# Sampling on 64-pixel blocks, regrouped per four image rows, with five or six candidate rows per tile

## The chip, the cores and the metric

The kernel runs on one core of a Trainium2 chip. The metric is the device time of one execution in microseconds (us); lower is better. Engines are named as in the profile: PE is TensorE's matmul, PEld its weight load, DVE is VectorE, ACT is ScalarE, POOL is GpSimd, SP issues most of the DMAs.

## What is computed

Four layers with a residual around each, on x of shape 2x192x96x96 in float32: a pair of deformable convolutions, an edge filter with a 1x1 merge, an RWKV layer and a Mamba layer. The change touches the first layer only:

```python
xr = conv1x1(gn(x), w_reduce, b_reduce)             # 192 -> 180 channels
offs = conv1x1(xr, w_offset, b_offset)              # 360: two convs, 10 groups x 9 taps x (y, x)
f_w = deform_conv2d(xr, offs[:, :180], w_dcnw, b_dcnw)
f_h = deform_conv2d(xr, offs[:, 180:], w_dcnh, b_dcnh)
# deform_conv2d: for each pixel, group and tap, sy = y + ky - 1 + dy, sx = x + kx - 1 + dx;
# val = bilinear sample of 18 channels of xr at (sy, sx), zero outside the image;
# out = einsum over taps and channels with the 3x3 weights
attn = softmax(conv1x1((f_w + f_h).mean(axis=(2, 3)), w_attn, b_attn))
x = x + conv1x1(attn[0] * f_h + attn[1] * f_w, w_expand, b_expand)
```

## The kernel before

Phases run one after the other: `first_norm_and_projections` (L153), `far_samples` (L367), `sample_and_convolve` (L652), `mix_and_expand`, and then the edge, RWKV and Mamba phases, which the change leaves alone.

**A bilinear sample as a matmul and a weighting.** A tile is 128 consecutive pixels; there are NT = 72 tiles per image and two images, 144 in all. For a tile and one of NB = 20 "samples" (two convolutions x 10 groups) each of the 9 taps needs 18 channels. The x-interpolation is a matmul: the stationary side is `HX`, for 96 image columns x 64 pixels the hat 1 - |x position - column| cut at zero; the moving side is `XW`, some image rows x 18 channels of xr over 96 columns. A tile holds pixels of two image rows, so for offsets up to 2.5 rows WIN = 6 candidate rows are taken: 6 x 18 = 108 columns. The y-interpolation is DVE's multiplication of the result by `HY`, the hats in y (`weigh`, L964 to L974). POOL adds the two halves of the six rows (`halve`, L889), DVE adds the remaining three in two steps (`quarter` L980, `sum_rows` L987). PE turns the values around (L859) and multiplies with the convolution weights (L872).

The matmul of a sample, two column halves of the array (o = 0 and 64) for the two halves of the tile:

```python
for t in range(TAPS):
    ky = t // 3
    for o in (0, 64):
        ins = e.matmul(PT[j % 2][o:o + 64, t // 3, (t % 3) * WIN * CG:(t % 3 + 1) * WIN * CG],
                       HX[:, m // 2 % RP, m % 2, t * 128 + o:t * 128 + o + 64],
                       XW[:, i, ky:ky + WIN, g * CG:(g + 1) * CG], ...)
```

**Order of the work.** Each engine has its own program, in an order written out by hand. `body` stands for four tiles (NRB = 4) and is a hardware loop of `nw` passes; nw is 1 if `far_samples` finds few enough samples with a larger offset. PE's step n (two samples a step, ten steps a tile): turn values of n; `sample(n+6)`, `sample(n+7)`; convolution matmuls of n. DVE's: `unload(n)` (copies what PE turned), a quarter of the next tile's `rows` (y distances, L934) at four of ten steps, `weigh(n+6)`, `quarter(n+4)`, `weigh(n+7)`, `sum_rows(n+4)`. PE's `sample(n+8)` waits until `weigh(n+6)` has emptied its PSUM buffer (PT has two), and the convolution matmuls wait for `unload(n)`. ACT makes the hats in x for pairs of samples, `distance` (L779) and `hats` (L784) on 96x2304 elements, seven and six pairs ahead of PE's step, and four small row-weight steps a tile (L795, L798), the first of which waits for DVE's `rows`. SP issues, for a pair, the broadcast load of the x positions into one of RP = 8 slots (`pair_load`, L743), which PE frees; before the ten pair loads of a tile stand the loads of y offsets (L724), of a distance table (L725) and of what far samples add (`CR`, L729; `KF`, L730), and among them the load of XW (L720) and the store of a finished tile (L737). POOL's `keep` (L906, L908) scales the kept sum ACC and adds CR.

**Far samples.** `far_samples` finds offsets outside the window (up to 8 candidates per partition, up to 128 in all), gathers their data with one indirect DMA per operand and adds their contribution into the `cor` array in DRAM. If there are more, nw becomes NWIN = 17 passes over all rows.

Of the kernel before, what the change touches and what calls it, by code (L numbers as in the profile page):

```python
# [18 lines left out]
NWIN = 17  # L19
# [5 lines left out]
PADT = 4  # L25
ROWS = 108
# [126 lines left out]
def first_norm_and_projections(nc, k):  # L153
# [4 lines left out]
    with Phase(nc, "in") as p:  # L158
# [34 lines left out]
        DT = p.sb([128, 3])  # L193
# [13 lines left out]
        with p.block() as blk:  # L207
            @blk.sync
            def _(e):
                for dst, src in ((WR[:, :, :], k.d["w_reduceT"].rearrange("(k p) o -> p k o", p=HC)),  # L210
                                 (WO[:, :, :, :], k.d["w_offT"].rearrange("(k p) t o -> p k t o", p=HM)),
                                 (BR[:, :], k.d["b_reduceT"]),
                                 (BO[:, :], k.d["b_offT"]), (DT[:, :], k.d["c_dlt"]), (BY[:, :], k.d["b_offy"][0:1, :].partition_broadcast(128)), (KX[:, :], k.d["c_kx"]), (PXR[:, :], k.d["c_pxr"])):
# [5 lines left out]
                for b in range(B):  # L219
                    for r0 in (0, PADT + H, PADT + H + 4):  # L220
                        e.dma_start(k.xr_v[b][r0:r0 + 4].rearrange("r p c -> p r c"), Z[:, :, :]).then_inc(s_zs, 16)
                for c, (b, r) in enumerate(chunks):
# [13 lines left out]
                e.wait_ge(s_zs, 16 * (6 + 2 * N)).then_inc(s_zs, -16 * (6 + 2 * N))  # L236

            @blk.scalar
            def _(e):
# [7 lines left out]
                def size(c):  # L247
# [3 lines left out]
                    for u in range(3):  # L251
                        ins = e.activation(AB[:, c % 3, u * CM:(u + 1) * CM], OY[:, c % 2, u, :], ACT.Abs,
                                           bias=DT[:, u:u + 1])
# [61 lines left out]
            def _(e):  # L315
                e.memset(Z[:, :, :], 0.0).then_inc(s_z, 1)
                for q in range(2):
                    e.sem_inc(s_st1[q], 16)
                    e.sem_inc(s_sx[q], 32)
# [13 lines left out]
                for c in range(N):  # L333
# [10 lines left out]
                    e.wait_ge(s_sx[q], 32).then_inc(s_sx[q], -32)  # L344
# [10 lines left out]
                for q in range(2):  # L355
                    e.wait_ge(s_st1[q], 16).then_inc(s_st1[q], -16)
                    e.wait_ge(s_sx[q], 32).then_inc(s_sx[q], -32)
# [9 lines left out]
def far_samples(nc, k):  # L367

    BIG = 1000.0
    SPARE = float(B * HW * 2)  # L370
    with Phase(nc, "far") as p:
        IOTA = p.sb([128, 8 * NCH0])
        PART = p.sb([128, 1])
        TRI = p.sb([128, 2, 128])
# [4 lines left out]
        CIF = p.sb([128, 8 * NCH0])  # L379
        EQ = p.sb([128, NCAND, 8 * NCH0])  # L380
# [4 lines left out]
        OH = p.sb([128, NCAND, 128])  # L385
        FL = p.sb([1, 4])
        Q = p.sb([128, 48])
        IN = p.sb([128, 1], I32)
        AD = p.sb([128, 8], I32)
        YX = p.sb([128, 2])  # L390
        XV = p.sb([128, 4, CG])
        WG = p.sb([128, CG * CM])
        WP = p.sb([128, CG * CM])
        VL = p.sb([128, CG])
        OUT = p.sb([128, CM])
        SUMS = p.sb([128, CM])
        RD = p.sb([128, 128])
        EM = p.sb([128, 128])
        EL = p.sb([128, 128])
# [3 lines left out]
        (s_w, s_v, s_cn, s_tot, s_oh, s_pay, s_ad, s_ix, s_rd, s_r, s_em, s_o, s_go) = p.sems(13)  # L403
# [2235 lines left out]
```

## Time and profile before

| what | us |
|---|---|
| median of 3 runs | 12407.22 (12399.02 to 12415.76) |
| profiled execution, its own time | 12423.67 |
| its span | 12421.6 |
| projections, about 86 to 455 | 369 |
| far samples and start of sampling, 455 to 548 | 93 |
| sampling, 548 to 7575 | 7027 |
| mix and expand, 7575 to 7837 | 262 |
| the other three layers, 7837 to the end | 4584 |

Busy over the span: PE 11555.8 us (93%), weight loads 8928.9 (72%), DVE 10330.4 (83%), ACT 10361.2 (83%), POOL 5958.3 (48%). How to read the rows: an instruction in float32 is issued as two on PE, so the 51,948 matmuls of L831 are 103,896 rows. The duration of one matmul is a latency that overlaps the next; what a stream costs is the distance of the starts. The rows on which the prediction rests stand further down.

### The profile page before, as it was taken

Reading aid. Unit: us, or ns where it says so; the run is one execution under the profiler, and the core shown is the slowest. Engines: PE = TensorE matmul, PEld = TensorE weight load, DVE = VectorE, ACT = ScalarE, POOL = GpSimd, SP = SyncE. Lnnn points to the kernel's source line nnn. Section 1 sums busy time; section 2 is a strip of 40 time slices with the busy share of each in tenths; the row PEclk is TensorE's granted clock in tenths of the full one; section 3 lists DMA queues with packets and bytes.
Section 4 is the critical chain, followed back from the end, with each engine's and each line's share of the span. In section 5 each row is a group of like instructions: output and inputs, shape, how many; then the busy total and the mean of one; then the engine's idle time right before and its main releaser. Section 6 shows DMA issues by size and latency. Waiting matters only on the chain. (4 is left out here: it accounts for less than half of the span.)

```text
span 12421.6 us, 338253 instructions
## 1 busy us (share of the span) xinstructions
PE 11555.8 (93%) x133056; PEld 8928.9 (72%) x133056; DVE 10330.4 (83%) x13907; ACT 10361.2 (83%) x10330; POOL 5958.3 (48%) x3910
## 2 busy tenths in 40 slices
PE   7699999999999999999999999880699899999999
PEld 4599999999999999999999996430533355555555
DVE  5588888888888888888888886799878788888888
ACT  3499899899998998989989885397768899899988
POOL 0155554455444545445454451033300388888887
PEclk9899999999999999999999997895899899999999
DMA  6688888888888888888888888444644333333332
GB/s 181 164 209 206 208 205 203 204 206 208 204 204 201 208 206 207 206 200 208 206 207 205 202 206 210 140 155 139 178 130 159 127 99 108 102 100 107 99 103 85
DMA packets 850969, 2144.79 MB, mean 173 GB/s; under 512 B 108322, under 2 KB 447184, under 8 KB 707168
## 3 DMA queue, kind: packets, MB, share of 16 engines
q1 hardware_dynamic: 833904, 2090.65, 63.7%
q10 hardware_dynamic: 15120, 30.71, 0.7%
q8 instruction: 1080, 17.69, 0.6%
q14 instruction: 481, 3.94, 0.1%
q0 software_dynamic: 384, 1.79, 0.0%
HBM read 1827.33 MB, written 295.56 MB: 171 GB/s over the span
## 5 line engine op out<-in xcount | busy, mean ns | idle before, releaser
L831 PE MATMUL dc_p<-dc_t 96*64 96x108 f32 x103896 | 5162.5, 257 | 85.9 <-issue 44.9
L831 PEld LDWEIGHTS dc_p<-dc_t 96*64 96x64 f32 x103896 | 4847.6, 136 | 353.6 <-issue 351.7
L900 POOL TENSOR_TENSOR dc_t<-dc_t 128x486 f32<-128x486 f32 x2885 | 3169.6, 1099 | 3525.6 <-DVEq L990 2344.8
L972 DVE TENSOR_TENSOR dc_t<-dc_p,dc_t 128x972 f32<-128x972 f32 x2886 | 3367.5, 1167 | 976.0 <-DVEq L970 880.4
L779 ACT ACTIVATE dc_t<-dc_t 96x2304 f32<-96x2304 f32 x1447 | 3191.8, 2206 | 222.3 <-ACTq L778 219.0
L784 ACT ACTIVATE dc_t<-dc_t 96x2304 f32<-96x2304 f32 x1446 | 3049.7, 2109 | 0.0
L2481 DVE TENSOR_TENSOR_SCAN ms_t<-ms_t,ms_p 128x512 f32<-128x512 f32 x1728 | 2128.5, 1271 | 282.9 <-PE ms_p L2423 203.5
L2397 POOL TENSOR_TENSOR ms_t<-ms_t 128x1536 f32<-128x1536 f32 x576 | 1987.9, 3457 | 503.5 <-DVE ms_t L2481 499.7
L2433 PE MATMUL ms_p<-ms_t,top_t 128*128 128x512 f32 x3456 | 1774.7, 596 | 0.0
L2423 PEld LDWEIGHTS ms_p<-top_t,ms_t 128*128 128x128 f32 x6912 | 849.7, 141 | 967.6 <-issue 693.1
L872 PE MATMUL dc_p<-dc_t 128*128 128x180 f32 (+1 forms) x7488 | 1537.0, 337 | 0.6 <-PEq L867 0.3
L872 PEld LDWEIGHTS dc_p<-dc_t 128*128 128x128 f32 (+1 forms) x7488 | 1139.2, 190 | 201.4 <-issue 4.0
L2369 ACT ACTIVATE ms_t<-ms_t 128x384 f32<-128x384 f32 x2304 | 1222.5, 603 | 24.2 <-PE ms_p L2423 24.2
L2376 ACT ACTIVATE ms_t<-ms_t 128x512 f32<-128x512 f32 x1728 | 1114.3, 709 | 0.0
L2423 PE MATMUL ms_p<-top_t,ms_t 128*128 128x128 f32 x6912 | 1048.3, 274 | 57.5 <-DVE ms_t L2481 51.1
L992 DVE TENSOR_TENSOR dc_t<-dc_t 128x324 f32<-128x324 f32 x1442 | 823.1, 571 | 0.0
L984 DVE TENSOR_TENSOR dc_t<-dc_t 128x324 f32<-128x324 f32 x1442 | 702.0, 487 | 0.2 <-DVEq L982 0.2
L959 DVE COPY dc_t<-dc_p 128x256 f32<-128x256 f32 (+1 forms) x1440 | 673.4, 468 | 9.1 <-DVEq L954 8.7
L859 PE MATMUL dc_p<-top_t,dc_t 128*128 128x128 f32 (+1 forms) x3744 | 646.3, 273 | 0.2 <-PEq L856 0.2
L795 ACT ACTIVATE dc_t<-dc_t 128x540 f32<-128x540 f32 x290 | 187.4, 646 | 535.3 <-ACTq L793 513.0
L934 DVE TENSOR_TENSOR dc_t<-dc_t 128x270 f32<-128x270 f32 x580 | 557.8, 962 | 71.6 <-DVEq L932 69.7
L2433 PEld LDWEIGHTS ms_p<-ms_t,top_t 128*128 128x128 f32 x3456 | 522.2, 191 | 15.8 <-DVE ms_t L2491 11.5
(256 smaller groups left out, 9864.2 us busy)
## 6 DMA issues: line engine op xcount, KB each, us to landing
dc_t<-sxd SPq DMA_DIRECT2D x1447, 864.0 KB, 5.9
ms_t<-bcd SPq DMA_DIRECT2D x576, 256.0 KB, 3.3
dc_t<-xrT SPq DMA_DIRECT2D x145, 540.0 KB, 9.0
kvd<-wk_t SPq DMA_DIRECT2D x18, 1536.0 KB, 5.1
szd<-mi_t SPq DMA_DIRECT2D x36, 768.0 KB, 4.4
xvd<-mi_t SPq DMA_DIRECT2D x36, 768.0 KB, 4.8
dld<-mi_t SPq DMA_DIRECT2D x36, 768.0 KB, 3.4
ms_t<-dld SPq DMA_DIRECT2D x36, 768.0 KB, 6.7
```

Source lines behind the costliest of these rows:

```text
L779: e.activation(HX[:, q % RP, :, :], HX[:, q % RP, :, :], ACT.Abs, bias=QX[:, 0:1]).then_inc(s_ab, 1)
L784: e.activation(HX[:, q % RP, :, :], HX[:, q % RP, :, :], ACT.Relu, bias=1.0, scale=-1.0)\
L831: ins = e.matmul(PT[j % 2][o:o + 64, t // 3, (t % 3) * WIN * CG:(t % 3 + 1) * WIN * CG], HX[:, m // 2 % RP, m % 2, t * 128 + o:t * 128 + o ...
L872: ins = e.matmul(PF[:, conv * CM:(conv + 1) * CM], VT[0:o, n // 2 % 2, u, :], WD[0:o, c, conv, :], start=(c == 0), stop=(c == NCK - 1), sk ...
L900: e.tensor_tensor(ZH[:, n % 4, :, :], z[:, :, 0:HALF], z[:, :, HALF:2 * HALF], ALU.add)\
L972: e.tensor_tensor(Zt[:, n % 4, :].rearrange("p (b m i) -> p b m i", b=3, i=CG), PT[n % 2][:, :, 0:3 * WIN * CG].rearrange("p b (m i) -> p ...
L2369: ins = e.activation(BU[:, i % RT, tb, :], UT[:, c % 2, tb, 0:DI], ACT.Copy, scale=UT[:, c % 2, tb, DI + n:DI + n + 1])
L2376: ins = e.activation(DA[:, i % RA, d, :], DL[:, c % 2, d, :], ACT.Exp, scale=AL[:, d, n:n + 1])
L2397: e.tensor_tensor(G[:, i % RG, :, :], HH[:, i % RH, :, :], CB[:, i % RB, :].unsqueeze(1).to_broadcast([128, ND, T]), ALU.mult).then_inc(s_ ...
L2423: ins = e.transpose(PB[:, d, tb * 128:(tb + 1) * 128], BU[:, i % RT, tb, d * 128:(d + 1) * 128], k.ident[:, :])
L2433: e.matmul(PY[:, d, :], k.ident[:, :], G[:, i % RG, d, :], start=(n == 0), stop=(n == NS - 1))\
L2481: e.tensor_tensor_scan(HH[:, i % RH, d, :], DA[:, i % RA, d, :], PB[:, d, :], CAR[:, n, d:d + 1], ALU.mult, ALU.add).then_inc(s_scan, 1)
```

## The change

**Tiles.** The 384 pixels of four image rows are six blocks of 64. Before, a tile is two neighbouring blocks: every tile touches two image rows. Now TILES pairs blocks (0, 2), (3, 5) and (1, 4). Blocks 0, 2, 3 and 5 each lie in a single image row; blocks 1 and 4 cross one. The first two tiles of three take five candidate rows (90 columns in place of 108), the third six. The two halves of a tile now read different rows of XW (BASES). XW holds ten rows for three tiles and is loaded once per three, in place of eight rows for each.

**Loop body.** NRB goes from 4 to 12 tiles, so the loops are 12 in place of 36.

**Sums.** `CR`, `KF` and POOL's `keep` go. `sum_load` loads ACC itself from `cor` and `sum_store` writes it back, one store of 180 KB per tile more; the load stands where CR's load stood. y offsets come in two DMAs of 64 partitions.

**Reach.** For single-row blocks the window covers offsets up to 2.0 either way (the test scales |dy| by 1.25), for the others as before. `far_samples` takes up to 256 in place of 128: most steps are made for two columns, gathers are doubled, there is one more gather (`c_spot`, where a pixel stands in its tile) that DVE waits for, one of the two big products goes to POOL, and both big sums stay on DVE. NWIN becomes 21.

**Around it.** The x positions are stored in six DMAs of 256-byte runs per chunk in place of two of 512-byte runs; four more stores of zero rows. `mix_and_expand` puts pixels back in order: four ACT instructions in place of two per chunk, six DVE instructions in place of two, over the same elements.

The core of the diff:

```diff
+TILES = ((0, 2), (3, 5), (1, 4))
+BASES = ((0, 1), (2, 3), (0, 2))
+ROWSOF = (5, 5, 6)
...
-                    for conv in range(2):
-                        e.dma_start(k.d["sxd"][b, 3 * r:3 * r + 3, conv].rearrange("i k x -> k i x"),
-                                    SX[:, q, conv, :].rearrange("k (i x) -> k i x", i=3)).then_inc(s_sx[q], 16)
+                        for i, (one, two) in enumerate(TILES):
+                            e.dma_start(k.d["sxd"][b, 3 * r + i, conv].rearrange("k (a x) -> k a x", a=2),
+                                        SX[:, q, conv, :].rearrange("k (n x) -> k n x", x=64)[:, one:two + 1:two - one, :])\
+                                .then_inc(s_sx[q], 16)
...
-    NRB = 4
+    NRB = 12
...
-                def kept_loads(i, b, ti, y):
-                    e.dma_start(CR[:, i, :], k.cor_v[DS(b * NT + y, 1)].rearrange("a p c -> (a p) c")).then_inc(s_cr[i % 2], 16)
-                    e.dma_start(KF[:, i:i + 1],
-                                k.d["c_keep"][DS(ti, 1)].rearrange("a p c -> (a p) c")).then_inc(s_cr[i % 2], 16)
+                def sum_load(i, at):
+                    e.wait_ge(s_sb, 16).then_inc(s_sb, -16)
+                    e.dma_start(ACC[:, i % 3, :, :].rearrange("p v c -> p (v c)"), k.cor_v[at]).then_inc(s_cr[i % 3], 16)
...
-                            if q == 0:
-                                tile_load(i, b, first)
+                            if q == 0 and i % 3 == 0:
+                                chunk_load(i, b, e.snap(near * (4 * (y // 3) + PADT - 6) + w * STEP + 3))
                             if q == 3:
...
                                 store_tile(i, done, s_st[i % 2])
+                                sum_store((i - 2) % 3, done)
...
-                        ky = t // 3
-                        for o in (0, 64):
-                            ins = e.matmul(PT[j % 2][o:o + 64, t // 3, (t % 3) * WIN * CG:(t % 3 + 1) * WIN * CG],
+                        for h in range(2):
+                            o, first = 64 * h, BASES[i % 3][h] + t // 3
+                            ins = e.matmul(PT[j % 2][o:o + 64, t // 3, t % 3 * nr * CG:(t % 3 + 1) * nr * CG],
                                            HX[:, m // 2 % RP, m % 2, t * 128 + o:t * 128 + o + 64],
-                                           XW[:, i, ky:ky + WIN, g * CG:(g + 1) * CG],
+                                           XW[:, i // 3 % 2, first:first + nr, g * CG:(g + 1) * CG],
...
-                    e.tensor_tensor(ZH[:, n % 4, :, :], z[:, :, 0:HALF], z[:, :, HALF:2 * HALF], ALU.add)\
+                    e.tensor_tensor(ZH[:, n % 4, :, 0:m], z[:, :, 0:m], z[:, :, nr * CG - m:nr * CG], ALU.add)\
                         .then_inc(s_half, 1)
-
-                def keep(i):
...
+                for h in range(2):
+                    gather(SPOT[:, h, :], k.d["c_spot"], 0, h, s_sp)
...
                 e.wait_ge(s_ix, 1)
-                for n in range(4):
-                    gather(XV[:, n, :], k.d["xrT"][0:B * ROWS].rearrange("r x (g i) -> (r x g) i", i=CG), 4 + n, s_xv)
+                for h in range(2):
+                    for n in range(4):
+                        gather(XV[:, h, n, :], k.d["xrT"][0:B * ROWS].rearrange("r x (g i) -> (r x g) i", i=CG), 4 + n, h, s_xv)
+                e.wait_ge(s_vl, 1)
+                e.wait_ge(s_wg, 32)
+                e.tensor_tensor(WP[:, 1, :].rearrange("p (i o) -> p i o", i=CG), WG[:, 1, :].rearrange("p (i o) -> p i o", i=CG),
+                                VL[:, 1, :].unsqueeze(2).to_broadcast([128, CG, CM]), ALU.mult).then_inc(s_wp, 1)
...
+                chained(e.tensor_reduce(OUT[:, 0, :], WP[:, 0, :].rearrange("p (i o) -> p o i", i=CG), AX.X, ALU.add))
+                e.wait_ge(s_wp, 1)
+                e.tensor_reduce(OUT[:, 1, :], WP[:, 1, :].rearrange("p (i o) -> p o i", i=CG), AX.X, ALU.add)\
+                    .then_inc(s_em, 1)
```

On PE, in the middle of the sampling loop, the order is the same and the width of L831's matmuls differs. `64x108` is 64 pixels by 6 x 18 columns. Before:

```order
L831 MATMUL dc_p<-dc_t 64x108 x36
L872 MATMUL dc_p<-dc_t 128x180 x3
L859 MATMUL dc_p<-top_t,dc_t 128x128 x2
L859 MATMUL dc_p<-top_t,dc_t 84x128
L831 MATMUL dc_p<-dc_t 64x108 x36
```

After, in a five-row tile:

```order
L884 MATMUL dc_p<-dc_t 64x90 x36
L925 MATMUL dc_p<-dc_t 128x180 x3
L912 MATMUL dc_p<-top_t,dc_t 128x128 x2
L893 MATMUL dc_p<-top_t,dc_t 90x128 x2
L884 MATMUL dc_p<-dc_t 64x90 x36
```

Nothing moved in it; 90 columns stand in place of 108. On SP, the DMAs of one tile in the loop, before (`sxd` are the pair loads, `xrT` is XW, `fd` the finished tile):

```order
L724 DMA dc_t<-oyd 128x180
L725 ISA
L725 DMA dc_t<-c_tab 128x6
L729 DMA dc_t<-cor 128x360
L730 ISA
L730 DMA dc_t<-c_keep 128x1
L743 DMA dc_t<-sxd 96x2304
L720 ISA
L720 DMA dc_t<-xrT 96x8x180
L743 DMA dc_t<-sxd 96x2304 x3
L737 DMA fd<-dc_t 90x4x128
L743 DMA dc_t<-sxd 96x2304 x6
```

After, a tile with the load of XW, the first of three:

```order
L772 DMA dc_t<-oyd 64x180 x2
L773 ISA
L773 DMA dc_t<-c_tab 128x6
L778 DMA dc_t<-cor 128x360
L794 DMA dc_t<-sxd 96x2304
L766 ISA
L766 DMA dc_t<-xrT 96x10x180
L794 DMA dc_t<-sxd 96x2304 x3
L784 DMA fd<-dc_t 90x4x128
L788 DMA cor<-dc_t 128x360
L794 DMA dc_t<-sxd 96x2304 x6
```

The table's load (`c_tab`) now stands behind two loads of y offsets, `c_keep` is gone, and the store into `cor` stands behind that of `fd`.

## Rows read from the trace of the kernel before

**Rows 1.** Stages: us, engines' busy us (PE, PEld, DVE, ACT, POOL), clock, DMA share, GB/s.
```profile
86.00:455.00 369.00, 360.85 (x1632) 233.04 (x1632) 188.24 (x386) 155.98 (x336) 0.00 (x0) 1.00 0.64 185
455.00:548.00 93.00, 6.35 (x24) 5.42 (x24) 49.97 (x154) 8.68 (x7) 7.84 (x8) 0.50 0.36 97
548.00:7575.00 7027.00, 6973.47 (x115704) 6487.65 (x115704) 5983.18 (x9079) 6337.75 (x3467) 3505.31 (x3173) 1.00 0.82 205
7575.00:7837.00 262.00, 249.88 (x412) 111.78 (x412) 152.97 (x306) 64.09 (x98) 0.09 (x1) 0.50 0.87 211
```

**Rows 2.** Groups by form, 548 to 7575 us: busy us, mean ns, idle before.
```profile
L831 PE MATMUL dc_p<-dc_t 96*64 96x108 f32 x103896 | 5162.5, 257 | 85.9 <-issue 44.9 <-PEq L827 39.6
L831 PEld LDWEIGHTS dc_p<-dc_t 96*64 96x64 f32 x103896 | 4847.6, 136 | 353.6 <-issue 351.7
L972 DVE TENSOR_TENSOR dc_t<-dc_p,dc_t 128x972 f32<-128x972 f32 x2886 | 3367.5, 1167 | 976.0 <-DVEq L970 880.4
L779 ACT ACTIVATE dc_t<-dc_t 96x2304 f32<-96x2304 f32 x1445 | 3187.4, 2206 | 217.2 <-ACTq L778 213.9 <-issue 0.3
L900 POOL TENSOR_TENSOR dc_t<-dc_t 128x486 f32<-128x486 f32 x2885 | 3169.6, 1099 | 3525.6 <-DVEq L990 2344.8 <-POOLq L896 891.2 <-POOLq L899 153.1
L784 ACT ACTIVATE dc_t<-dc_t 96x2304 f32<-96x2304 f32 x1446 | 3049.7, 2109 | 0.0
...
L795 ACT ACTIVATE dc_t<-dc_t 128x540 f32<-128x540 f32 x288 | 186.1, 646 | 450.8 <-ACTq L793 428.6 <-ACTq L791 22.3
```

**Rows 3.** Timeline of PE, one step of sampling: start us, us from first to end.
```profile
5015.25 3.55 PE L831 MATMUL dc_p<-dc_t 96*64 96x108 f32 x72
5018.73 1.18 PE L872 MATMUL dc_p<-dc_t 128*128 128x180 f32 x6
...
5020.06 3.55 PE L831 MATMUL dc_p<-dc_t 96*64 96x108 f32 x72
```

**Rows 4.** Timeline of PE in the projections, matmuls of other widths.
```profile
299.91 0.63 PE L300 MATMUL in_p<-top_t,in_t 90*128 90x90 f32 x6
300.38 2.75 PE L282 MATMUL in_p<-in_t 90*90 90x384 f32 x8
302.96 1.99 PE L291 MATMUL in_p<-in_t 90*128 90x180 f32 x12
304.79 2.75 PE L274 MATMUL in_p<-in_t 96*90 96x384 f32 x8
```

**Rows 5.** Timeline of weight loads: the first four of a run of samples.
```profile
3001.41 0.20 PEld L831 LDWEIGHTS dc_p<-dc_t 96*64 96x64 f32 x4 [0.17 <-issue]
```

**Rows 6.** Waits of PE, DVE and ACT, 560 to 7570 us: total us, times, longest.
```profile
PE dc_p L831 <- issue: 44.2, 45, 2.6
...
DVE dc_t L934 <- DVEq L932: 60.5, 81, 2.1
...
ACT dc_t L795 <- ACTq L793: 428.6, 144, 3.8
```

**Rows 7.** DMA issues, 1000 to 7000 us: count, KB each, median us to landing.
```profile
dc_t<-sxd SPq DMA_DIRECT2D x1233, 864.0 KB, 5.9
...
dc_t<-c_tab SPq DMA_DIRECT2D x124, 3.0 KB, 5.3
```

**Rows 8.** Timeline of SP: one load of y offsets is issued.
```profile
523.98 0.33 SPq L724 DMA_DIRECT2D dc_t<-oyd  x1
```

**Rows 9.** Groups in the far phase, 455 to 548 us.
```profile
L432 POOL DMA_INDIRECT far_t<-xrT,far_t x4 | 3.8, 944 | 11.9 <-DVE far_t L611 11.0 <-issue 0.9
L422 PE MATMUL far_p<-far_t 128*128 128x4 f32 x16 | 3.6, 355 | 11.5 <-DVE far_t L502 11.5
```

**Rows 10.** Timeline of DVE in the far phase, the end of its chain.
```profile
502.32 0.24 DVE L457 TENSOR_SCALAR far_t<-far_t 128x18 f32<-128x18 f32 x1 [4.44 <-DMA far_t<-xrT,far_t]
...
503.41 3.53 DVE L463 TENSOR_TENSOR far_t<-far_t 128x3240 f32<-128x3240 f32 x1
506.98 6.77 DVE L633 TENSOR_REDUCE far_t<-far_t 128x180 f32<-128x3240 f32 x1
```

More of the change, by code:

```diff
@@ L419, in _ @@
                 e.matmul(PA[:, 2:4], ONES[:, :], CN[:, :], start=True, stop=True).then_inc(s_tot, 1)
                 e.wait_ge(s_oh, 1)
-                for n in range(NCAND):
-                    ins = e.matmul(PB[:, 0:4], OH[:, n, :], PAY[:, n, :], start=(n == 0), stop=(n == NCAND - 1))
+                for h in range(2):
+                    for n in range(NCAND):
+                        ins = e.matmul(PB[:, 4 * h:4 * h + 4], OH[:, n, h * 128:(h + 1) * 128], PAY[:, n, :],
+                                       start=(n == 0), stop=(n == NCAND - 1))
@@ L445, in _ @@
[L445 removed]
+                for h in range(2):
+                    e.indirect_dma_start(k.d["cor"], bass.IndirectOffsetOnAxis(ap=AD[:, 8, h:h + 1], axis=0), SUMS[:, h, :],
+                                         None).then_inc(s_cor, 16)
+                e.wait_ge(s_cor, 32)
             @blk.vector
@@ L550, in _ @@
-                floor(delta, t0, t1)
-                pairs(delta, delta, u, ALU.subtract)
-                scale(spare, PART[:, :], 1.0, SPARE)
-                combine(row, px, 2.0, conv)
+                scale(spare, PART[:, :], 1.0, SPARE)
+                tile, place, base, delta, centre, reach = (SPOT[:, :, n] for n in range(6))
+                e.wait_ge(s_sp, 32)
+                combine(row, c, 3.0, tile)
+                combine(t1, row, 2.0, conv)
+                combine(t1, t1, float(HM), gt)
@@ L635, in _ @@
                 scale(t1, b, -1.0, 1.0)
+                pairs(ey, t1, t0, ALU.mult)
+                pairs(sx, t1, conv, ALU.mult)
+                pairs(dy, b, t0, ALU.mult)
+                pairs(dx, b, conv, ALU.mult)
+                e.wait_ge(s_xv, 128)
+                for h in (1, 0):
+                    scale(VL[:, h, :], XV[:, h, 0, :], ra[:, h:h + 1], None, ALU.mult, ALU.bypass)
+                    combine(VL[:, h, :], XV[:, h, 1, :], rb[:, h:h + 1], VL[:, h, :])
+                    combine(VL[:, h, :], XV[:, h, 2, :], xa[:, h:h + 1], VL[:, h, :])
+                    ins = e.scalar_tensor_tensor(out=VL[:, h, :], in0=XV[:, h, 3, :], scalar=xb[:, h:h + 1],
+                                                 in1=VL[:, h, :], op0=ALU.mult, op1=ALU.add)
+                    if h == 1:
+                        ins.then_inc(s_vl, 1)
+                    else:
+                        chained(ins)
@@ L2620, in layout @@
-    d["c_dlt"] = (pu // W - np.arange(3) - REACH + 2).astype(f)
+    block, base, single = (np.zeros((3, 2, 64), np.int64) for _ in range(3))
+    for i in range(3):
+        for h in range(2):
+            block[i, h], base[i, h], single[i, h] = TILES[i][h], BASES[i][h], ROWSOF[i] == 5
+    at = (64 * block + np.arange(64)).reshape(3, 128)
+    base, single = base.reshape(3, 128), single.reshape(3, 128)
+    row = at // W
+    r = np.arange(WIN)
+    tab = np.zeros((2, H // 4, 3, NWIN, 128, WIN), f)
```

402 lines of the change are left out of this document (216 added, 186 removed).

## Prediction, made before the changed kernel was run

> **What bounds the kernel now.** I read the stages first [rows 1]. Sampling takes 7027 us of 12421.6, and in it PE is busy 6973 us, ACT 6338, DVE 5983, POOL 3505, with the DMA engines at 0.82. So per tile (7027 / 144 = 48.8 us) PE has almost no air; ACT fills 6338 / 144 = 44.0 us, DVE 41.5. The groups by form [rows 2] say what PE does there: the 103,896 issued matmuls of L831, 36 per sample. The waits confirm the bound from the other side: DVE and ACT wait for their turn [rows 2, 6], while PE's L831 has 85.9 us of idle time in the stage, 44.2 of them put down to "issue" in 45 gaps.
>
> A busy PE need not be a PE that is bound by columns, so I read distances of starts. One step, two samples, is 72 instructions in 3.55 us [rows 3]. Without the last one's latency (257 ns, rows 2) that is 3.29 / 71 = 46.4 ns each, 92.8 ns per pair, a pair being the instruction of the left half and that of the right. In the projections, where a matmul uses the whole array width, the starts give 0.47 / 6 = 78 ns for 90 columns, 1.83 / 12 = 152.5 for 180 and 2.58 / 8 = 322.5 for 384 [rows 4]: 2.5 ns + 0.833 ns per column. For 108 columns that line gives 92.5 ns. So two halves together cost what one costs alone, the weights are loaded under the stream, and the columns set the pace. The clock is at its upper level, 2.4 GHz, in this stage (1.00 in rows 1). A whole step lasts 4.81 us [rows 3], ten make 48.1 us a tile; the last 0.7 us of the 48.8 are the start and scattered stalls.
>
> **Sampling matmuls.** Width 108 becomes 90 in two tiles of three, 96 tiles. By the line a pair goes from 92.5 to 77.5 ns; the 78 ns for exactly 90 columns [rows 4] stands for it too. 15 ns x 18 pairs = 0.27 us per sample, x 20 = 5.4 us per tile, x 96 = **518 us** off PE's path. A five-row tile then takes 42.7 us on PE, a six-row tile 48.1, the mean is 44.5.
>
> Could the weight loads hold the pace? In the trace four loads, 136 ns each [rows 2], fit into 0.20 us [rows 5], so two pairs start within 64 ns: a pair of loads can follow every 55 to 64 ns, under 77.5. I take the columns. The Trainium skill (TensorE: Matmul & The Clock Gate, section "LDWEIGHTS (loading the stationary operand)") gives a load about its columns / 1.2 in ns, 53 for 64 columns. Two of them in turn would be 107 ns per pair, and the narrower matmul would save nothing (the second rival's 12,435 us); the trace, at 92.8 per pair, disagrees with loads in turn and agrees with loads of both halves side by side.
>
> **What is late next.** ACT: 44.0 us per tile; its small steps shrink from 540 to 450 elements, by the slope between 2304 and 540 elements (2109 and 646 ns, rows 2) 75 ns each, 0.3 us a tile. So it needs 43.7 in a five-row tile against PE's 42.7, 44.0 in a six-row one against 48.1. In three tiles it needs 131.4 us, PE 133.5. Its 428.6 us of waiting at L795 [rows 6], 3 us a tile, are where it stands ahead of DVE's `rows`; it is three pairs, about 12.8 us, ahead of PE there and loses 2 us of that in two tiles. So it hides, narrowly: 0.7 us a tile. DVE: 41.5 us less 20 products shortened by 162 elements, at (3.53 - 1.167) / (3240 - 972) = 1.04 us per thousand elements [rows 2, 10] 0.17 each, gives 38.1 of 42.7. POOL halves 324 for 486 elements and loses `keep`; it had air. DMA: 10.0 MB a tile by rows 1 (205 GB/s x 48.8 us). XW falls from 540 to 675 / 3 = 225 KB, the store of ACC adds 180, its load replaces CR's: 9.87 MB in 44.5 us, a share of 0.82 x 0.987 x 48.8 / 44.5 = 0.89. A pair load lands in 5.9 us [rows 7] and has about six steps of 4.3 us, less some 8 us for ACT and its order; hidden.
>
> **The wait that grows.** DVE's first `rows` of a tile waits for the table, which lands 5.3 us after its issue [rows 7]: 60.5 us in 81 tiles [rows 6], 0.4 us a tile. One more issue of 0.33 us [rows 8] stands ahead of it now, and PE's step is 0.54 us shorter, so it is late by up to 1.3 us. Behind it on DVE stands `weigh(n+6)`, for which PE's sample two steps on waits. DVE's idle time shrinks from 976 / 1440 = 0.68 us a step [rows 2] to 4.6 / 10 = 0.46. One step can't absorb 1.3 us, but PE needs the result only a step later. Bounds: 0, and 0.9 us per five-row tile (all but one step's air), 86 us. With the "issue" gaps (44 us now, with more DMA load perhaps twice) I take 40 us in all, nearer to 0 since the order gives DVE a step of lead, and 0 to 130 for the range.
>
> **Sums and loop.** `sum_load` waits for the store of the tile before, issued seven pair loads (30 us) earlier: no wait. Behind it on SP stand pair loads with the air above. POOL's `keep` was hidden. 24 loop ends fewer: nothing in the trace shows that one costs PE, 0, at best a part of the 44 us.
>
> **Far samples**, an exposed chain while PE is idle (6.35 of 93 us busy, rows 1). Doubling adds: four more gathers before the wait of 4.44 us, 0.94 and 0.3 of issue each [rows 9, 10], 5.0 us; 16 more candidate matmuls, 3.6 [rows 9]; a second reduction on DVE, 6.8 [rows 10]; four small products, 1.0, four more sums of 180 elements at 0.34, 1.4, the wider one-hot, 1.1 (at 1.04 per thousand); one more scatter, 1.25; one more constant, about 1; DVE's new waits for `c_spot` and for the second address, between 0 and 4.4 each, 3.4 together. The second product, on POOL, 3240 x 1.099 / 486 = 7.3 us, is under DVE's own 3.5 + 6.8. Sum 24.6, **25 us**, range 15 to 40. The samples are a matter of data: worked out from the inputs, 119 lie outside the new windows (67 the old ones), at most 6 in one partition; 256 and 8 are allowed. It stays one pass.
>
> **Projections.** PE is busy 361 of 369 us [rows 1]. SP issues four more stores per 7.5 us chunk, at 0.33 to 0.85 us: room. DMA: x positions are 270 of 1390 KB per chunk; even if their share tripled, 0.64 would become 0.88. Hidden, but at the end some 2 us. The Trainium skill (DMA: Bandwidth & Descriptors, section "Specifications") wants 512 bytes and more per transfer and has smaller ones do a read-modify-write, which speaks against runs of 256; no row here shows such a store, and by the bound above it would stay hidden. **Mixing**: PE is busy 250 of 262 us at clock 0.50, DVE 153, ACT 64 [rows 1]. Four more DVE instructions per chunk at a fixed 0.16 us (the line above at 0 elements) are 0.6 of 2.3 us of idle time: 0. Start of sampling: 1 us.
>
> **Sum.** -518 + 40 + 25 + 2 + 1 = -450 us. On the profiled execution, 12423.7, that is 11974; it stands 16.5 us above the median of the runs, so **11957 us**, 3.6% faster.
>
> **Rivals.**
> - *The wait that grows and ACT, uncovered.* ACT's lead or DVE's step doesn't hold: each lost 0.3 to 0.9 us per tile, together 43 to 130 more than I took: 12,000 to 12,090. For it: 0.7 us of air on ACT, 0.46 on DVE. Against it: the leads. 21%.
> - *Something else than columns sets the pair.* Then only the added work is left: 12407 + 28 = 12,435, slower. It decides from a pair of 91.7 ns on, where 34,560 pairs save less than 28 us. Against it: the straight line through 78, 152.5 and 322.5, and 92.8 on it. 5%.
> - *The halves no longer run side by side*, since they read different rows of XW where they read the same. Pairs of 155 and 185 ns: 22.5 and 33.3 us more per tile, mean 26.1, 16,200 us. The starts in rows 3 are of the same rows, so no row excludes it. 2%.
> - *Too many far samples*: 21 passes. The count excludes it; with all else 1%.
> - *More than the columns.* The start and the stalls shrink, or mixing runs at the upper clock, where DVE would bound it at 0.16 us x 192 + 153 = 184 us: 11,840 to 11,905. 9%.
>
> **How the numbers follow.** My forecast with its neighbourhood, 11,905 to 12,000: 62%. Range: 11,885 to 12,055, which leaves out the slower ones and the edges of the two near ones. 0.2% is 25 us, about what a measurement of this kernel can tell from no change. Faster by more: 62 + 21 + 9 = 92%; within: 2% (part of the second rival); slower: 6%.
>
> **What would show it.** Right: L884's 72 instructions of a five-row step in about 3.0 us (71 x 38.8 + 0.25); sampling near 6550 us, five-row tiles 43, six-row 48; ACT's wait at its first row weight nearly gone; the far stage near 118 us. Wrong: the run of 72 at 3.5; PE waiting for the x hats or for `weigh`'s buffer; gaps put down to "issue" well above 80 us.

## The result, and the profile after

| | before | after |
|---|---|---|
| median of the runs, us | 12410.11 (12399.02 to 12415.76) | 12071.65 (12053.83 to 12096.23) |
| profiled execution, us | 12423.67 | 12053.83 |
| its span, us | 12421.6 | 12051.9 |

The change makes the kernel 2.7% faster: the ratio is 0.973, with a 95% interval from 0.971 to 0.9749. The direction was forecast, the size was not. 12071.65 us lies 115 us above the predicted 11957 and 17 us beyond the end of the range.

The stages of the kernel after, in the form of [rows 1] (us, busy us of PE, PEld, DVE, ACT and POOL, granted clock, DMA share, GB/s):

```profile
88.00:505.00 417.00, 381.71 (x1632) 238.00 (x1632) 190.88 (x386) 172.69 (x336) 0.00 (x0) 0.97 0.61 167
505.00:631.00 126.00, 11.99 (x46) 10.63 (x46) 67.44 (x166) 7.84 (x7) 22.94 (x19) 0.50 0.31 86
631.00:7219.00 6588.00, 6474.64 (x115704) 6009.03 (x115704) 5426.72 (x9080) 6287.46 (x3467) 2591.75 (x2885) 0.99 0.84 216
7219.00:7482.00 263.00, 249.88 (x412) 111.83 (x412) 177.58 (x497) 90.75 (x194) 0.00 (x0) 0.51 0.88 210
```

Sampling is 439 us shorter, mixing is what it was, and the two stages ahead of sampling are longer than in [rows 1]: the projections by 48 us, the far samples by 33. So the sum of the prediction can be laid beside the two profiled executions, stage by stage:

| stage | predicted, us | measured, us |
|---|---|---|
| load of x and statistics | 0 | +1.6 |
| projections | +2 | +47.4 |
| far samples | +25 | +33.5 |
| start of sampling | +1 | +0.5 |
| sampling, first to last product on DVE | -518 + 40 | -439.2 (7023.0 to 6583.8) |
| mixing | 0 | +1 |
| code that the change doesn't touch | 0 | -14 |
| sum | -450 | -370 |

The remaining 34 us of the miss of 115 have nothing to do with a mechanism. The prediction took the profiled execution as 16.5 us above the median of its runs; that of after stands 18 below its own. The row of untouched code is scatter between executions: over the changed kernels' profiles it lies between -3 and -18 us.

**The columns.** PE's groups in sampling, and one five-row step of its timeline (start us, us from first to end):

```profile
L884 PE MATMUL dc_p<-dc_t 96*64 96x90 f32 x69152 | 2935.2, 242 | 90.0 <-issue 54.3 <-PEq L879 34.1
L884 PE MATMUL dc_p<-dc_t 96*64 96x108 f32 x34560 | 1713.7, 257 | 18.0 <-issue 17.4 <-PEq L879 0.3
```

```profile
3007.04 3.01 PE L884 MATMUL dc_p<-dc_t 96*64 96x90 f32 x72
```

The 72 instructions take 3.01 us where [rows 3] has 3.55. (3.01 - 0.24) / 71 is 39.0 ns each, 78 per pair, as the line through [rows 4] said. The halves still run side by side though they now read different rows of XW. The best tiles last 42.6 and 42.9 us with five rows, 47.7 with six, and 48.0 before.

**What stands around them.** The waits in sampling, 640 to 7215 us, in the form of [rows 6]:

```profile
DVE dc_t L979 <- DVEq L977: 240.9, 143, 8.7
```

```profile
ACT dc_t L847 <- ACTq L845: 177.2, 126, 3.3
ACT dc_t L831 <- ACTq L830: 98.1, 124, 3.9
```

L979 is `rows`, DVE's y distances, and L977 its wait for the y offsets and the table; L847 is the first of ACT's row weights, which waits for `rows`, and L831 ACT's `distance`, which waits for a pair load. `rows` waited 60.5 us in 81 tiles [rows 6]; it now waits 240.9 in 143 of 144. The idle time of PE's two groups above is 108 us, from 85.9 [rows 2]; these are only the gaps that the profile sees. ACT is busy for 6287 of the stage's 6588 us, so at this point it could as well be ACT that holds the pace. That is what the second group of experiments separates.

**The projections.** SP's queue in one chunk of 384 pixels, first of before, then of after:

```profile
304.50 0.40 SPq L231 DMA_DIRECT2D xrT<-in_t  x1
304.94 1.02 SPq L234 DMA_DIRECT2D sxd<-in_t  x2
306.00 0.93 SPq L226 DMA_DIRECT2D cor<-in_t  x2
306.97 0.70 SPq L228 DMA_DIRECT2D oyd<-in_t  x1
```

```profile
301.38 0.98 SPq L235 DMA_DIRECT2D xrT<-in_t  x1
302.41 5.34 SPq L239 DMA_DIRECT2D sxd<-in_t  x6
307.79 1.03 SPq L230 DMA_DIRECT2D cor<-in_t  x2
308.87 0.44 SPq L232 DMA_DIRECT2D oyd<-in_t  x1
```

Before, SP issues for 3.2 us and then waits for the next chunk. After, it issues back to back: from xrT at 301.38 to the next xrT at 309.43 are 8.05 us, while PE needs 7.46 for a chunk. DVE's operation L353, which makes the x positions, waits for the chunk's buffer, filled two chunks earlier and not yet stored. Its waits, 110 to 480 us:

```profile
DVE in_t L353 <- DVEq L351: 109.1, 46, 4.4
```

L351, named here, is the wait for PE's result; it stands just behind L350, the wait for the buffer. From the fifteenth chunk on L351 passes 0.11 us after L350 (309.21 and 309.10 us in the chunk above), so there it is the buffer that ends last.

The stage's extra 47 us come apart by the starts of DVE's copy L349 (L343 before), 48 of each. The first comes 5 us later than the 1.6 of the load explain, and the second another 6.4 later; in this stretch PE's matmuls run at half their pace (last section). Over the following chunks the distance is 7.46 us for thirteen chunks and 8.16 on average for the 33 from then on, some 25 us more than before in all. At the end, 20 us in place of 9 lie between the last copy and the far stage, since SP is behind.

### The profile page after: what moved, and what is told of

It is laid out like the page before. It is cut to its first block and busy times, and to the rows that moved or that the text cites. A ratio compares the mean times of both kernels' runs of the same rounds, so it can differ in the third digit from the quotient of the medians.

```text
span 12051.9 us, 337397 instructions
## 1 busy us (share of the span) xinstructions
PE 11074.3 (92%) x133078; PEld 8457.9 (70%) x133078; DVE 9815.6 (81%) x14111; ACT 10353.3 (86%) x10426; POOL 5059.6 (42%) x3633
## 5 line engine op out<-in xcount | busy, mean ns | idle before, releaser
L884 PE MATMUL dc_p<-dc_t 96*64 96x90 f32 (+1 forms) x103896 | 4658.9, 247 | 144.9 <-issue 71.7
L884 PEld LDWEIGHTS dc_p<-dc_t 96*64 96x64 f32 x103896 | 4370.8, 136 | 418.1 <-issue 416.4
L955 POOL TENSOR_TENSOR dc_t<-dc_t 128x324 f32<-128x324 f32 (+1 forms) x2885 | 2591.8, 898 | 4028.3 <-DVEq L1043 2738.2
L1019 DVE TENSOR_TENSOR dc_t<-dc_p,dc_t 128x810 f32<-128x810 f32 (+1 forms) x2886 | 3043.5, 1055 | 896.4 <-DVEq L1016 861.1
L831 ACT ACTIVATE dc_t<-dc_t 96x2304 f32<-96x2304 f32 x1447 | 3189.0, 2204 | 105.6 <-ACTq L830 104.5
L1045 DVE TENSOR_TENSOR dc_t<-dc_t 128x324 f32<-128x324 f32 x1442 | 730.8, 507 | 0.0
L979 DVE TENSOR_TENSOR dc_t<-dc_t 128x225 f32<-128x225 f32 (+1 forms) x580 | 410.2, 708 | 250.6 <-DVEq L977 250.4
L912 PEld LDWEIGHTS dc_p<-top_t,dc_t 128*128 128x128 f32 (+1 forms) x3744 | 496.2, 140 | 18.9 <-issue 1.4
L1034 DVE TENSOR_TENSOR dc_t<-dc_t 128x324 f32<-128x324 f32 x962 | 465.2, 484 | 0.4 <-issue 0.2
```

What stands on the lines that cost most here:

```text
L831: e.activation(HX[:, q % RP, :, :], HX[:, q % RP, :, :], ACT.Abs, bias=QX[:, 0:1]).then_inc(s_ab, 1)
L884: ins = e.matmul(PT[j % 2][o:o + 64, t // 3, t % 3 * nr * CG:(t % 3 + 1) * nr * CG], HX[:, m // 2 % RP, m % 2, t * 128 + o:t * 128 + o + 6 ...
L912: ins = e.transpose(PR[0:o, u * 128:(u + 1) * 128], VA[:, n // NG % 2, 128 * c:128 * c + o], k.ident[:, :])
L955: e.tensor_tensor(ZH[:, n % 4, :, 0:m], z[:, :, 0:m], z[:, :, nr * CG - m:nr * CG], ALU.add)\
L1019: e.tensor_tensor(Zt[:, n % 4, 0:nr * LEN].rearrange("p (b m i) -> p b m i", b=3, i=CG), PT[n % 2][:, :, 0:3 * nr * CG].rearrange("p b (m ...
```

## Experiments

Two theories stood at each of two places. All kernels are the changed one with one edit, unless told otherwise. Medians are compared with 12071.65 us for the changed kernel; ratios are to the kernel before, on the same chip.

### What sets a chunk of the projections

**p_zeros_act.** The same stores, but two of a chunk's ten are issued by ACT:

```diff
 SyncE:   for c, (b, r) in enumerate(chunks):
 ...
-             for i in (2 * c, 2 * c + 1):
-                 e.dma_start(k.cor_z[i], Z...).then_inc(s_zs, 16)
 ScalarE:
+         e.wait_ge(s_z, 1)...
          for c in range(N):
+             for i in (2 * c, 2 * c + 1):
+                 e.dma_start(k.cor_z[i], Z...).then_inc(s_zs, 16)
```

> The changed kernel, with the two zero stores of the sums of every chunk (96 in all) issued by ScalarE in place of SyncE; the same packets go the same way at about the same time. Theory A (SyncE's time for issuing its DMAs sets the chunk in the projections: 0.97 + 6 x 0.87 + 0.57 + 0.42 + 0.44 us and gaps, 8.03 in all, against 7.46 that TensorE needs): the sum falls to about 7.0, the period of a chunk returns to 7.46, and the projections end some 25 to 30 us sooner, near 477 in place of 505.6; the time falls by as much, to about 12045. Theory B (the DMA engines set it, with twice as many descriptors of 256 bytes in place of 512): the period stays at 8.0 to 8.1 and the time at 12070.

Measured: 12039.45 us (12032.78 to 12056.33), ratio 0.9704 (0.9683 to 0.9725). The distance of the chunks is 7.46 us from the first to the last. The projections end at 461.3 us in place of 506.2, 45 us sooner; 12 of them are the slow start, which this execution didn't have. Against the kernel before, the stage is 4 us longer.

```profile
88.00:450.00 362.00, 360.60 (x1632) 232.84 (x1632) 183.93 (x375) 167.90 (x334) 0.00 (x0) 1.00 0.67 189
```

PE is busy 360.6 of 362 us again, and the DMA engines move 189 GB/s in place of 167. The same packets, issued from two queues, go through faster. Each of the six stores still holds SP for 0.87 us, though SP now pauses in every chunk, so that figure isn't one of a crowded queue. So it was SP's issue time, theory A, and not the DMA engines.

**p_two_stores.** DVE writes the x positions in the order of the tiles, and two stores take the place of six:

```diff
-    for i, (one, two) in enumerate(TILES):
-        e.dma_start(sxd[b, 3 * r + i, conv] (k, a, x), SX[:, q, conv] blocks one and two)
+    e.dma_start(sxd[b, 3 * r:3 * r + 3, conv] (k, i, x), SX[:, q, conv] (k, i, x))
```

> The changed kernel, with the x offsets of a chunk laid in the order of the tiles by VectorE (6 operations of 128 columns in place of 2 of 384), so that two stores with runs of 512 bytes take the place of six with runs of 256. Theory A: SyncE's issues come to about 3.5 us a chunk, the period returns to 7.46, the projections end near 462 to 470 (the four added stores of zero rows stay), and the time falls by 36 to 44 us, to about 12030. Theory B gives the same here, since the descriptors are halved as well; a period above 7.46 would mean that neither holds and that the larger VectorE work or something else sets it. Far samples and sampling are unchanged by either.

Measured: 12039.68 us (12029.21 to 12050.96), ratio 0.9704 (0.9684 to 0.9724). The distance is 7.46, and the projections end at 455.7 us. DVE's 25 us of extra work in the stage (209.0 of 362 us busy) cost nothing. This edit alone would not have told the theories apart. It shows that SP's 36 us can be had back; that the other 11 are missing here too is chance, since best_a has the same stores and the slow start, and its stage is 12 us longer than before.

The two traces have sampling stages of 6605 and 6599 us, 21 and 15 longer than the profiled execution of after, and the medians fell by 32 where the stage gave 45 and 50. What lengthened sampling there was not tried; with the loads early as well, in best_a, it takes 6462 us, so the two stores don't do it by themselves.

### What sets the five-row tiles

**s_early_rows.** The loads for `rows` of tile i + 1 stand behind the fifth pair load of tile i in place of behind its tenth:

```diff
-    row_loads(i, b, ti, y)
+    if i == 0:
+        row_loads(i, b, ti, y)
     sum_load(i, 2 + b * NT + y)
     for q in range(10):
         pair_load((10 * i + q) % RP, b, y, q)
+        if q == 4 and i + 1 < NRB:
+            row_loads(i + 1, b, e.snap(t0 + w + (y + 1) * NWIN), y + 1)
```

> The changed kernel, with the y offsets and the row table of a tile (three DMAs) issued five pairs earlier, in 132 of 144 tiles. Theory C (in sampling these loads land too late for VectorE's row sums, which hold up VectorE and through it ScalarE's row weights and TensorE): VectorE's wait at the row sums falls from 241 us to under 40, ScalarE's wait for them from 177 to under 60, sampling from 6584 us to about 6450 (144 tiles at the best seen, 42.6 and 47.7, are 6379), and the time by 100 to 150. Theory D (ScalarE's own work, 43.7 us a tile on average against TensorE's 44.3, sets it; its waits are those of an engine that could not have gone ahead): the waits move elsewhere and the time falls by less than 30.

Measured: 11944.97 us (11942.5 to 11957.15), ratio 0.9628 (0.9609 to 0.9648), 127 us less. Sampling takes 6467 us. The same waits, now over 700 to 6900 us (in that window the changed kernel has 221.8 at `rows` and 169.6 at ACT's row weights):

```profile
ACT dc_t L834 <- ACTq L833: 85.6, 102, 2.9
ACT dc_t L850 <- ACTq L848: 78.7, 58, 3.0
PE dc_p L887 <- issue: 30.5, 45, 1.7
...
DVE dc_t L982 <- DVEq L980: 11.1, 11, 1.8
```

The wait at `rows` is left in 11 tiles, those at the head of the loop whose loads the edit doesn't move. PE's gaps, and ACT's wait for the row sums, went with it. That is theory C; 117 of the 127 us are in sampling.

**s_less_act.** ACT's second pass works on half of the elements (every second sample's column weights are left out):

```diff
-    e.activation(HX[:, q % RP, :, :], HX[:, q % RP, :, :], ACT.Relu, bias=1.0, scale=-1.0)
+    e.activation(HX[:, q % RP, 0, :], HX[:, q % RP, 0, :], ACT.Relu, bias=1.0, scale=-1.0)
```

> The changed kernel with the second of ScalarE's two passes over a pair's columns made on half of them; the column weights of every second sample are left out by that. ScalarE has some 10 us less work in a tile. Theory D (ScalarE's work): tiles of five rows come to the best seen, 42.6 us, and sampling to about 6400, 150 to 190 us less. Theory C (late loads alone): VectorE's wait at the row sums stays near 240 us and sampling falls by less than 60. If both have a part, between the two.

Measured: 12072.49 us (12046.73 to 12094.0), ratio 0.9733 (0.9712 to 0.9755); sampling 6583.9 us against 6583.8.

```profile
ACT dc_t L831 <- ACTq L830: 1072.4, 790, 4.7
...
ACT dc_t L847 <- ACTq L845: 373.9, 136, 4.3
DVE dc_t L979 <- DVEq L977: 228.2, 134, 4.3
```

ACT now stands still for nearly a quarter of that window, and not a microsecond comes of it. Its full timetable was no bound: it was busy because it was ahead. Theory D falls.

**s_early_less_act**, both edits, asks the same of what the early loads left over.

> The changed kernel with the early loads and with ScalarE's second pass on half the columns (the column weights of every second sample are left out). What the early loads left above the floor is 6467 - 6379 = 88 us. Theory D2 (with the loads in time, ScalarE, which stands still for only 168 of 6467 us, is what is left): sampling falls by 50 to 90 more, to about 6400, and the time to 11870. Theory E (the rest is TensorE's own gaps and VectorE's order): sampling stays at 6455 to 6470 and the time at 11945.

Measured: 11949.06 us (11932.83 to 11963.21), ratio 0.9625 (0.961 to 0.964); sampling 6467.8 us. ACT is not the rest either. The five- and six-row tiles at their best, 44.4 us on average, would make 6405 us (144.25 tiles from first to last product, an estimate from the trace); some 62 us stay above that. By position in the loop they are spread over all tiles, 0.1 to 0.8 us each. What makes them was not found.

**s_six_rows.** All tiles with six rows, the regrouping kept:

```diff
     def depth(n):
-        return ROWSOF[n // NB % 3]
+        return WIN
```

and the same in `row_weights` and `rows`, with one row more in XW.

> The changed kernel with six rows on all three tiles (the weights of the sixth row are zero where the change leaves it out): the regrouping, its stores, loads, sums in memory and far samples stay, the 15% fewer columns go. If the gain of sampling is that of the columns alone and the regrouping is free, sampling takes what it took before, 7023 us, within 30, at 48.0 a tile at best, and the time is 12071 + 439 = 12510, slower than before by 0.8%. If the new loads cost something of their own besides, sampling takes 7060 to 7130. Theory C says that the wait at the row sums is much smaller here than 241 us, 60 to 120, since a pair takes 0.5 us longer and the loads have more time.

Measured: 12468.54 us (12460.76 to 12471.47), ratio 1.0039 (1.0024 to 1.0055). Sampling takes 6986 us, 37 less than before, with best tiles of 48.0. Of the 42 us by which my figure was too high 37 are these; the rest is not accounted for.

```profile
DVE dc_t L979 <- DVEq L977: 104.7, 116, 2.5
```

This run takes the sampling term apart. Against a floor of 144.25 tiles of 48.0 us, 6924, the kernel before had 99 us of stalls and this one 62: regrouping is no cost but a small gain. Six rows to five lowers the floor by 519 us, to 6405, and raises the stalls from 62 to 179. The early loads take them back to 62. So the lateness of these loads cost 117 us. By this account nearly all of it appeared only with the shorter step, though the third DMA was there with six rows too, and with it 104.7 us of wait at `rows` (49.2 in the kernel before, same window). Six rows with the loads early, which would have shown this directly, was not run.

**before_early** puts the loads five pairs earlier in the kernel before, in three of four tiles.

> The kernel before, with the y offsets and the table loaded five pairs earlier in three of four tiles. Theory C, that the load's lateness was there before and the shorter tile uncovered it: the wait at the row sums (60.5 us) nearly goes, and sampling falls by no more than those 60, likely 20 to 50, to about 6985; the time to about 12375. If the lateness came only with the change (a third DMA in a row's loads), nothing moves: 12410.

Measured: 12383.39 us (12369.2 to 12402.43), ratio 0.9972 (0.9959 to 0.9985); sampling 6986 us, 37 less.

```profile
DVE dc_t L937 <- DVEq L935: 15.1, 22, 1.9
```

The lateness was there before the change. Over 560 to 7570 us the wait falls from 60.5 [rows 6] to 16.4, and sampling gets 37 us shorter for these 44.

**s_one_pair** moves the loads by one pair only (`q == 8` in place of `q == 4`).

> The changed kernel with the loads of y offsets and table only one pair earlier (ahead of the last pair's load of the tile before) in place of five. If lateness is all there is to it, a step of 4.3 us covers most of a wait that is 1.7 us a tile on average and 8.7 at worst: the wait at the row sums falls from 236 us to 20 to 60, sampling from 6584 to 6470 to 6510, and the time to about 11965 to 11990. If the five pairs did something else besides (spread the loads away from the chunk's load and the stores, which stand at fixed places of the tile), one pair gives less than half of the 127 us.

Measured: 11947.99 us (11942.65 to 11962.35), ratio 0.9624 (0.9607 to 0.9642); sampling 6462.6 us.

```profile
DVE dc_t L982 <- DVEq L980: 9.0, 12, 1.4
```

One step of 4.3 us gives everything that five give (124 us and 127, with overlapping intervals). I had taken the wait as the lateness in every tile, with 8.7 us at worst, and so expected a rest of 20 to 60 us; but the 8.7 us is one tile at the start of the stage, and elsewhere the longest is 4.6.

**s_one_load.** The two DMAs of y offsets become one over both blocks:

```diff
-    for h in range(2):
-        at = 384 * (y // 3) + 64 * TILES[y % 3][h]
-        e.dma_start(OYT[64 * h:64 * h + 64, i % 2, :], k.oyd_v[b][at:at + 64])
+    src = k.oyd_v[b][384 * (y // 3):384 * (y // 3) + 384].rearrange("(n x) c -> n x c", x=64)
+    e.dma_start(OYT[:, i % 2, :], src[one:two + 1:two - one])
```

> The changed kernel with the y offsets of a tile loaded by one DMA over both halves in place of two, at their old place. With six rows the new loads waited 105 us where the kernel before waited 60.5, so the third DMA is put at some 45 us of wait: if it is its issue (0.55 us) and landing in a row that counts, the wait at the row sums falls from 236 to 150 to 200 us, sampling by 30 to 70 us and the time to about 12020. If the same bytes land as late through one DMA, nothing moves: wait 220 to 250, 12070.

Measured: 12386.8 us (12348.44 to 12399.3), ratio 0.9971 (0.9961 to 0.9982). This is 315 us slower than the changed kernel, and both of my expectations were wrong. Sampling takes 6880 us, and even the best five-row tile lasts 44.2.

```profile
DVE dc_t L979 <- DVEq L977: 471.1, 131, 5.0
ACT dc_t L847 <- ACTq L845: 439.4, 130, 5.7
PE dc_p L884 <- PEq L879: 221.7, 167, 3.2
```

The packets of 720 bytes say why. In one tile of the changed kernel the two DMAs' 128 packets start within 1.05 us (3034.25 to 3035.3), with 7 under way at a time. In this kernel the 128 packets of the tile at 3037 us take from 3041.3 to some 3044, with 2.2 under way at a time on average. The Trainium skill (DMA: Bandwidth & Descriptors, section "Why a DMA increments its semaphore by 16 and not by 1") has the rule: the number of engines is the largest up to 16 that divides the slowest dimension of both sides. The slowest dimension of this DMA's source is 2, so it would use two of the 16 DMA engines; with two DMAs it is 64, which 16 divides. The trace agrees, with 2.2 packets under way against 7. (It doesn't say on which engine a packet ran.)

**s_one_load_early** asks whether the two crowded engines do harm beyond the late data.

> The changed kernel with the y offsets of a tile in one DMA and, with the table, five pairs earlier. The one DMA at the old place cost 315 us. Theory F (its data only land later, since its 128 packets go two at a time and take 2.7 us in place of 1.05, and the row sums wait for them): issued five pairs earlier, the lateness is gone, the wait at the row sums is under 20 us, sampling 6465 us and the time 11945, as with two DMAs. Theory G (the packets crowded on few DMA engines hold up the pair loads behind them): the wait at the row sums goes, but the pair loads stay late, the best tile stays above 43.5 us and the time is 12050 to 12250.

Measured: 11945.67 us (11932.52 to 11956.86), ratio 0.961 (0.9592 to 0.9627); sampling 6470 us, best tiles of 42.6 again. Theory F holds: all 315 us were the wait at `rows`. In the one at the old place that wait is 3.6 us a tile (471.1 over the 130 tiles of the window) where the changed kernel has 1.6 (221.8 over 136), and the 2.0 us of difference are the 2.1 by which a tile is longer there. A DMA whose data are not awaited may be as clumsy as this one for nothing.

### All together

**best_a**: early loads, two stores, and the far samples' second product on DVE.

```diff
 GpSimd:
-    e.wait_ge(s_vl, 1)
-    e.tensor_tensor(WP[:, 1], WG[:, 1], VL[:, 1] broadcast, ALU.mult).then_inc(s_wp, 1)
 VectorE, ahead of the second reduction:
-    e.wait_ge(s_wp, 1)
+    pairs(WP[:, 1], WG[:, 1], VL[:, 1] broadcast, ALU.mult)
```

> The changed kernel with three edits together: the y offsets and the table of a tile five pairs earlier, the x offsets stored with two DMAs a chunk in the order of the tiles, and the second product of the far samples on VectorE in place of GpSimd. If the gains add: 127 us of the early loads, some 44 of the stores (projections end 50 us sooner in that trace), and 2 of the product (3.5 us on VectorE in place of the 5.5 us for which its 0.24 us operation stood still beside GpSimd's product), so 11945 - 44 - 2 = about 11900. If ScalarE or the queue takes part of one of them back, 11915 to 11945. In the far stage itself: if VectorE stands still because of GpSimd's operation, the step from the loaded values to the last sum falls from 24.5 us by about 2; if the 5.5 us were a wait for something else, it rises by 3.5.

Measured: 11902.9 us (11896.65 to 11904.68), ratio 0.9586 (0.9573 to 0.9599). It beats both kernels, by 507 and 169 us (517 against the kernel before on its own chip). The gains add up. In its far stage, from the loaded values to the last reduction:

```profile
531.23 0.24 DVE L482 TENSOR_SCALAR far_t<-far_t 128x18 f32<-128x18 f32 x1 [7.26 <-DMA far_t<-xrT,far_t]
...
533.41 3.53 DVE L488 TENSOR_TENSOR far_t<-far_t 128x3240 f32<-128x3240 f32 x1
536.97 6.77 DVE L673 TENSOR_REDUCE far_t<-far_t 128x180 f32<-128x3240 f32 x1
543.78 3.53 DVE L488 TENSOR_TENSOR far_t<-far_t 128x3240 f32<-128x3240 f32 x1
547.34 6.77 DVE L676 TENSOR_REDUCE far_t<-far_t 128x180 f32<-128x3240 f32 x1
```

From 531.23 to the end of the last reduction the step takes 22.9 us where it took 24.5: DVE does 3.5 us more work and is done 1.6 us sooner.

## Why the prediction was wrong

The miss is 115 us. The projections make 45 of them, the stalls of sampling 39, the far samples 8.5, the level of the medians 34; the small terms and the untouched layers take 12 back.

**The bound and the columns: right.** PE and its columns set sampling. The term was 518 us; the best tiles of six-row and five-row kernels are 519 apart over the stage. A pair of 77.5 ns was forecast, 78 found; the rivals of another bound and of halves in turn are excluded.

**The projections: the step that failed.** "SP issues four more stores per 7.5 us chunk, at 0.33 to 0.85 us: room." The room was never added up. With SP's own issues before (0.40 + 1.02 + 0.93 + 0.70, some 3.2 us with its gaps) four more at 0.85 would have made 6.6 of 7.46, so even the sum would have said "just fits". What it missed is that the four are not added to two at 0.5: all six cost 0.87 on average, 5.3 us, and xrT's issue went from 0.40 to 0.97. The two kinds of store of x positions are 180 runs of 256 bytes and 270 of 512, so the smaller store is the dearer one. With 8.05 us against 7.46 and two buffers, the queue sets the chunk. I had bounded the DMA engines (0.88), which ended at 0.61, and treated SP as if only its engines counted. p_zeros_act shows this: eight issues on SP and two on ACT, same bytes, and the stage is back but for 4 us. Of the 47 us, 36 are SP's (25 and its being behind at the end), and 11 the slow start, of which nothing in the prediction spoke. I also weighed the rule of the Trainium skill (DMA: Bandwidth & Descriptors, section "Specifications") against runs under 512 bytes and put it aside as hidden. Its direction shows in the packets of the stage (130 to 430 us), and so does that it was hidden: one of 256 bytes takes a DMA engine 18.3 ns in p_zeros_act, one of 512 bytes 31.1 in p_two_stores, so the short runs cost 18% more engine time for the same bytes, and PE waits in neither. A read-modify-write is not to be seen in a trace.

**The stalls: the mechanism right, the size wrong.** The wait at `rows` was named, with its cause (a DMA more, a shorter step) and its place on DVE. It was priced at 40 us, with the reason that DVE's order leaves PE a step of lead; the net is 80, made of 37 gained by the regrouping, which the prediction gave nothing, and 117 lost by the lateness. The wrong part is the lead: 1.25 us of waiting a tile more (240.9 - 60.5 over 144 tiles) became 0.8 us of tile time, nearly two thirds, where I had let one step absorb all but a little. before_early shows the same of the kernel before: 37 us of time for 44 of wait. My own upper bound, 86 us for this wait, was too low as well.

**ACT uncovered: wrong as a rival, and rightly not the forecast.** The first rival joined the late loads and ACT's 0.7 us of air. The time came out inside its interval, 12,000 to 12,090, but with one half of its mechanism only: s_less_act and s_early_less_act gave ACT far more air and moved nothing. And 45 of the 115 us come from the projections, outside that rival. That the time fell into its interval is luck.

**The far samples: sized inside the range (33.5 in 15 to 40), with one term wrong.** "The second product, on POOL, is under DVE's own 3.5 + 6.8." It was not beside anything:

```profile
569.15 5.59 POOL L466 TENSOR_TENSOR far_t<-far_t 128x3240 f32<-128x3240 f32 x1 [3.59 <-DVE far_t L669]
```

```profile
569.25 5.80 DVE L487 SCALAR_TENSOR_TENSOR far_t<-far_t 128x18 f32<-128x18 f32 x2
575.09 0.24 DVE L669 SCALAR_TENSOR_TENSOR far_t<-far_t 128x18 f32<-128x18 f32 x1
```

Two DVE operations of 18 elements, 0.51 us together in the first half of the step (568.29 us) and in best_a, take 5.80, and end 0.3 us after POOL's product does. That is 5.3 us of the 8.5 missing. The Trainium skill (SBUF — State Buffer, section "SBUF: two separate sides") says that VectorE with two SBUF inputs and GpSimd (where GpSimd's instruction reads SBUF, as this one does) share a port pair as an exclusive lock, held for the whole instruction; the trace agrees, by 5.3 us.

**Mixing, start, sums and loop: right.** 263 us against 262 and 0.5 us for the start; nothing in the traces shows a cost of `sum_load` or of the added work in mixing, and one pass was enough for the far samples.

**The range.** It gave the projections 2 us and nothing either way, and took the profiled execution as 16.5 us above the median on both sides. The first error is a term without bounds. The second is 34 us by itself, twice the 17 by which the time lies beyond the range.

## What to carry to other kernels

Where a change splits DMAs, add up the issue time of the queue for one period, with the measured duration of the nearest shape and one at twice that, and compare it with the period as one does for an engine; if it is close, spread the issues over another queue. A load that lands just as it is needed should go one step earlier before the step is shortened: its wait looks small as long as the step hides it, and moving it by one step cost one condition and gave 124 us. An engine that is full in the profile and ahead of its consumer is not a bound; halving its work is a cheap way to know.

## What the runs showed of the hardware

- The issue time of a DMA on SP doesn't follow its bytes. 135 KB as 270 runs of 512 bytes took 0.49 us (p_two_stores), 45 KB as 180 runs of 256 bytes 0.87 (the changed kernel), and a pair load of 864 KB 0.30.
- A DMA whose slowest dimension is 2 had 2.2 packets under way at a time: 128 packets in 2.8 us in place of 1.05 (s_one_load against the changed kernel).
- 256 bytes as one packet took 18.3 ns of a DMA engine, 512 bytes 31.1 (means of the stores in the projections of p_zeros_act and p_two_stores).
- A POOL operation of 5.59 us on SBUF held up a DVE operation with two SBUF inputs for 5.3 us.
- In 8 of the 11 profiles of changed kernels, and in neither of the two of the kernel before (with its loads early or not), the matmuls of the first one or two chunks of the projections came 640 ns apart in place of 320 for 384 columns, the pace of 1.2 GHz in place of 2.4, and it cost 12 us (one chunk) or 19 (two). The other profiles have this pace too, but only for the first 4 us. The page gives the granted clock as 1.00 there, but the trace's first record of it is the step to 1.00, and stands at 118.7 us in the changed kernel and at 118.2 in best_a, against 90.5 in p_two_stores; ahead of it nothing is recorded. PE had been idle for 10 us before the first matmul in both. p_two_stores and best_a are the same up to this point, and show both (88 to 118 us, mean ns after the busy time):

```profile
L278 PE MATMUL in_p<-in_t 96*90 96x384 f32 x35 | 13.7, 538 | 0.0
```

```profile
L278 PE MATMUL in_p<-in_t 96*90 96x384 f32 x24 | 15.9, 843 | 10.2 <-PEq L275 10.2
```

  So it isn't the edit that makes it. What does was not tried.
